# A four-layer graph network on one core: border tiles are kept in SBUF and scattered last, instead of being gathered twice

## The reference

```
L0, four steps:  m = (h @ W_msg.T + b).reshape(n, 4, 128)
                 r = segment_sum(m[src, etype], dst);   h = GRU(r, h)
L1:              pe = relu(edge_w @ pos_w1) @ pos_w2
                 s = segment_sum(pe * x[src] + x[src], dst); agg = s / max(cnt, 1)
                 out = relu(batchnorm(concat(x, agg) @ sage_w + b)) + x
L2:              messages = segment_sum(h[src] @ W_msg.T + b + emb[etype], dst);  h = GRU(messages, h)
L3:              attention over the edges of each node with 8 heads, skip, norm, feed-forward
```

## Time and profile before

| | |
|---|---|
| time, median of 3 runs | 4368.6 us (4366.22 to 4368.82) |
| profiled execution | 4371.13 us, its span 4369.0 us |
| TensorE | 2877.3 us busy, 66% of the span |
| VectorE | 1801.5 us, 41% |
| ScalarE | 442.1 us, 10% |
| GpSimd | 2838.1 us, 65% |
| mean granted TensorE clock | 0.816 |
| gathers | 1612 in L0, 806 in L1 and L2, 416 in L3 |

### The profile page before, as it was taken

One profiled execution on the slowest core, in us unless ns is written; L12 is line 12 of the kernel. 1 busy time (PEld: TensorE's weight loads), 2 busy tenths in 40 slices (PEclk: granted clock), 3 DMA queues, 4 the chain that ended last, 5 costly groups with the idle time before them and its releaser, 6 DMA issues. The chain is left out here.

```text
span 4369.0 us, 45184 instructions
## 1 busy us (share of the span) xinstructions
PE 2877.3 (66%) x12174; PEld 2171.4 (50%) x12175; DVE 1801.5 (41%) x4737; ACT 442.1 (10%) x719; POOL 2838.1 (65%) x2971
## 2 busy tenths in 40 slices
PE   6565576555765567666667777776555866664697
PEld 3444444444444444444446666644444455654574
DVE  5222242222422224444453333432222666667874
ACT  3000020000200002000011111120000211111333
POOL 5777767777677776777746777557777277775000
PEclk9777787777977778877888999977777888887799
DMA  4112221212221222122212111112112155553340
GB/s 168 52 52 52 53 87 52 53 52 52 88 52 53 53 52 87 53 52 52 52 30 70 52 52 52 40 48 52 53 52 52 47 154 157 157 157 108 106 144 15
DMA packets 143872, 313.44 MB, mean 72 GB/s; under 512 B 49875, under 2 KB 64410, under 8 KB 143290
## 3 DMA queue, kind: packets, MB, share of 16 engines
q0 software_dynamic: 97344, 213.17, 18.1%
q1 hardware_dynamic: 46458, 99.48, 6.5%
HBM read 250.83 MB, written 61.63 MB: 72 GB/s over the span
## 5 line engine op out<-in xcount | busy, mean ns | idle before, releaser
L584 POOL DMA_INDIRECT ring<-m_tab,idx x1612 | 1535.0, 952 | 521.5 <-issue 489.6
L1535 PE MATMUL ps<-nodes,ring 128*128 128x256 f32 (+1 forms) x2816 | 897.2, 483 | 509.6 <-DMA ring<-m_tab,idx 399.1
L1535 PE MATMUL ps<-oh,ring 128*128 128x256 f32 (+1 forms) x2852 | 891.3, 476 | 475.9 <-DMA ring<-m_tab,idx 376.7
L1535 PEld LDWEIGHTS ps<-nodes,ring 128*128 128x128 f32 x2816 | 643.8, 252 | 657.8 <-issue 553.0
L1535 PEld LDWEIGHTS ps<-oh,ring 128*128 128x128 f32 x2852 | 647.8, 250 | 625.5 <-issue 518.1
L584 POOL DMA_INDIRECT ring<-x_tab,idx x806 | 766.6, 951 | 254.4 <-issue 238.9
L1022 DVE TENSOR_SCALAR oh<-iota,dl 128x256 f32<-128x256 f32 x1223 | 373.2, 375 | 941.0 <-PE ps L1535 940.3
L1022 DVE TENSOR_SCALAR nodes<-iota,dl 128x256 f32<-128x256 f32 x1200 | 366.7, 376 | 856.0 <-PE ps L1535 856.0
L584 POOL DMA_INDIRECT ring<-kv_tab,idx x416 | 401.3, 965 | 133.2 <-issue 126.5
L594 POOL TENSOR_TENSOR small<-small,bc 128x4 f32<-128x4 f32 (+1 forms) x28 | 29.6, 1057 | 452.5 <-DVE small L1121 452.5
L1535 PE MATMUL ps<-wpad,rts 128*128 128x128 f32 x832 | 157.1, 366 | 179.8 <-DVE pw L1312 179.8
(11 more groups left out here) (257 smaller groups left out, 2524.7 us busy)
## 6 DMA issues: line engine op xcount, KB each, us to landing
ve_dr<-pw SPq DMA_DIRECT2D x52, 512.0 KB, 3.0
ring<-ve_dr SPq DMA_DIRECT2D x52, 512.0 KB, 3.4
ring<-m_tab,idx POOLq DMA_INDIRECT x1612
m_tab<-ring SPq DMA_DIRECT2D x75, 256.0 KB, 2.1
ring<-x_tab,idx POOLq DMA_INDIRECT x806
ring<-kv_tab,idx POOLq DMA_INDIRECT x416
nodes<-in_xT SPq DMA_DIRECT2D x2, 1600.0 KB, 13.5
kv_tab<-nodes SPq DMA_DIRECT2D x25, 128.0 KB, 1.7
```

The costliest lines, as they stand in the source:

```text
L584: pool.indirect_dma_start(rows[:, j, :], None, table, bass.IndirectOffsetOnAxis(ap=idx[:, wave * WV + j:wave * WV + j + 1], axis=0)).then_ ...
L1535: return T.matmul(o, lhsT, rhs, start=start, stop=stop, skip_group_check=True)
```

## The change

The second gather of border tiles goes away: 391 gathers a pass in the six passes before L3.

ScalarE copies every landed tile out of its ring slot into one of 20 places in the half of `ring` that these passes leave free: a tile that crosses a border goes to the place of that border, any other to one of eight places that each wave writes over. The column of the place comes from a table (`kept_at`) over `load_kept`. TensorE waits for a wave's copies (`kept`) before its last tile (in L1, before the second half), so that the credit covers them. In L1 the copies are made of the finished messages, four after each half wave.

Wave 48 now has seven tiles, four on the slot's semaphore and three on `gat_end`. Two waves without gathers follow, 49 with eight border tiles and 50 with four. Their one-hots are built like those of other waves, with buffers of their own for the last waves. Behind the last of them VectorE moves the twelve border tiles to fixed rows (`move_borders`), and TensorE scatters each when it is moved (`borders`), in the order of banks. `evac` no longer waits for the whole pass: bank c goes when border 2c is scattered (`border`), the last with the credit; L1 keeps the old rule. In L0 the first matmul of `gru` waits for banks 0 to 2 only, L2 for all.

At the start TensorE has a matmul more (`later`) and VectorE fourteen steps more, on one partition, that work out the places: two ahead of the border records, twelve behind `i_iob`, ahead of the table adds L1148. Since `kept_at` lies in `cols_b`, the three steps that fill `cols_b` for L3 move from before L2's pass to behind L2's update, ahead of L3's first one-hots.

```diff
-P_WAVES = -(-P_SLOTS // WV)
-P_LAST = P_SLOTS - (P_WAVES - 1) * WV
+M_WAVES = -(-TILES // WV)
+M_LAST = TILES - (M_WAVES - 1) * WV
+M_FIRST = 4
+P_WAVES = M_WAVES - (-P_EXTRA // WV)
...
+        def bank_done(eng, k, c):
+
+            if c == NCH - 1 or l1(k):
+                eng.wait_ge(credit, first_wave(k + 1) + DEPTH)
+            else:
+                eng.wait_ge(border, k * (NCH - 1) + c + 1)
...
             def gathers(k, table, width, idx):
-                waves, deep, slots = (WAVES, RING, SLOTS) if single(k) else (P_WAVES, DEPTH, P_SLOTS)
+                waves, deep, slots = (WAVES, RING, SLOTS) if single(k) else (M_WAVES, DEPTH, TILES)
...
-                        ).then_inc(gat[u], 16)
+                        ).then_inc(gat_end if not single(k) and wave == M_WAVES - 1 and j >= M_FIRST else gat[u], 16)
...
             def evac(k):
-                act.wait_ge(credit, first_wave(k + 1) + DEPTH)
                 for c in range(1, NCH, 2):
                     c0, cw = CH[c]
+                    bank_done(act, k, c)
...
+            def keep(r, j, rows, last=False):
+
+                ins = nc.scalar.activation(ring_flat[:, ds(r[j], P)], rows[:, j, :], ACT.Copy)
+                if last:
+                    ins.then_inc(kept, 1)
+
+            def keep_tiles(k):
+
+                def wave(i, u, g, n):
+                    if isinstance(g, int) and g >= M_WAVES:
+                        return
+                    r = load_kept(act, kept_at, mybir.EngineType.Activation, first_slot(g), n)
+                    arrived(act, k, i, u, g)
+                    act.wait_ge(kept, k * M_WAVES + i * DEPTH + u + 1)
+                    for j in range(n):
+                        if n == M_LAST and j == M_FIRST:
+                            last_arrived(act, k)
+                        keep(r, j, wave_rows(g, u), j == n - 1)
...
             def relus(i, waves):
...
                         nc.scalar.activation(pw[:, hf, :], ps[:, 7, :], ACT.Relu).then_inc(l1_relu, 1)
+                        act.wait_ge(l1_msg, q + 2)
+                        if hf == 0:
+                            act.wait_ge(kept, PASS_L1 * M_WAVES + i * DEPTH + u + 1)
+                        for j in range(4 * hf, min(n, 4 * hf + 4)):
+                            keep(r, j, wave_rows(wave, u), j == n - 1)
...
+            def move_borders(k):
+
+                at = load_kept(dve, border_at, mybir.EngineType.DVE, 0, P_EXTRA)
+                dve.wait_ge(kept, (k + 1) * M_WAVES + 1)
+                for b in range(P_EXTRA):
+                    V.tensor_copy(border_rows(b), ring_flat[:, ds(at[b], P)]).then_inc(moved, 1)
...
+            def borders(k, wave, counting=False):
+
+                u, n, b0 = wave - LOOPED * DEPTH, tiles_of(wave), (wave - M_WAVES) * WV
+                pe.wait_ge(oh_ready, first_wave(k) + wave + 1)
+                for j in range(n):
+                    c0 = (b0 + j + 1) * PAIR
+                    pe.wait_ge(moved, k * P_EXTRA + b0 + j + 1)
+                    ins = mm(psf[:, c0:c0 + PAIR], border_rows(b0 + j), pair_oh(k, u, wave, j), start=False, stop=False)
+                    if (b0 + j) % 2 == 0:
+                        ins.then_inc(border, 1)
...
+                ins.then_inc(credit, 1)
...
             def sums(k, counting=False):
...
+                        if j == n - 1:
+                            tiles_kept(k, i * DEPTH + (u + 1))
...
-            def evacuated(k):
+            def evacuated(k, first=False):
                 def f(c=0):
-                    if c == 0:
+                    if c == 0 and first:
+                        pe.wait_ge(ev_d, k * EV_D + 2)
+                        pe.wait_ge(ev_a, k * EV_A + 1)
+                    elif c == 0 or c == 1 and first:
```

More of the change, by code:

```diff
@@ L83, in load_cols, with load_kept @@
         skip_runtime_bounds_check_because="window starts are multiples of 128 under 3200 by construction")[1]
+def load_kept(eng, row, which, start, n):
+    return eng.bass.values_load_multi_w_load_instructions(
+        row[0:1, ds(start, n)], engines=[which], min_val=P, max_val=(P_EXTRA + WV - 1) * PAIR + P,
+        skip_runtime_bounds_check_because="the column of one of 20 places for tiles")[1]
 def load_both(pe, row, wave):
@@ L116, in tiles_of, with first_slot, in_first @@
 def tiles_of(wave):
-    return P_LAST if isinstance(wave, int) and wave == P_WAVES - 1 else WV
-IN_SLOT = [16 * sum(tiles_of(wave) for wave in range(s, P_WAVES, DEPTH)) for s in range(DEPTH)]
+    if not isinstance(wave, int) or wave < M_WAVES - 1:
+        return WV
+    return M_LAST if wave == M_WAVES - 1 else min(WV, P_EXTRA - (wave - M_WAVES) * WV)
+def first_slot(wave):
+    if not isinstance(wave, int) or wave < M_WAVES:
+        return wave * WV
+    return TILES + (wave - M_WAVES) * WV
+def in_first(wave):
+    return M_FIRST if wave == M_WAVES - 1 else WV
+IN_SLOT = [16 * sum(in_first(wave) for wave in range(s, M_WAVES, DEPTH)) for s in range(DEPTH)]
 def landed(k, s, i, n=WV):
@@ L255, in build @@
         gat = [sem(f"gat{i}") for i in range(max(DEPTH, RING))]
+        gat_end = sem("gat_end")
+        kept = sem("kept")
+        border = sem("border")
+        moved = sem("moved")
         mt_mm = sem("mt_mm")
@@ L372, in build, with pair_oh, l1 @@
         oh_half = [oh[:, b, :, :].rearrange("p s c -> p (s c)") for b in range(2)]
[L373 to L377 removed]
+        oh_half += [gT[:, 1024 * b:1024 * (b + 1)] for b in range(3)] + [rec_flat[:, 3600:4624], oh_x]
+        END_HALVES = {M_WAVES - 1: (4, 6), M_WAVES: (0, 1), M_WAVES + 1: (5,)}
+        def pair_oh(k, u, wave, j):
+            half = 2 * (u % OH_BUFS) + j // 4
+            if isinstance(wave, int) and (wave > M_WAVES or wave >= M_WAVES - 1 and not l1(k)):
+                half = END_HALVES[wave][j // 4]
+            return oh_half[half][:, (j % 4) * PAIR:(j % 4 + 1) * PAIR]
+        def l1(k):
+            return isinstance(k, int) and k == PASS_L1
         def slot(s):
@@ L429, in whole_turns @@
                 turn(i, [i * DEPTH + u for u in range(DEPTH)])
-            turn(LOOPED, [LOOPED * DEPTH + u for u in range(P_REST)])
+            turn(LOOPED, list(range(LOOPED * DEPTH, M_WAVES)))
         def new_state(unit, eng, r, c, h_in, h_out):
@@ L719, in relus @@
                 for u, wave in enumerate(waves):
-                    for hf in halves(wave):
+                    n = tiles_of(wave)
+                    r = load_kept(act, kept_at, mybir.EngineType.Activation, first_slot(wave), n)
+                    for hf in range(2):
                         q = (i * DEPTH + u) * 2 + hf
@@ L985, in _ @@
             step("w_c16", V.tensor_scalar(cols16[:, :], cols2[:, :], 3, None, ALU.arith_shift_right))
+            after_g = pw[0:1, 1, 0:TILES + 1]
+            is_border = pw[0:1, 2, 0:TILES]
+            in_wave = pw[0:1, 3, 0:M_WAVES * WV]
+            n_before, lower, n_lower, none = (small[0:1, q:q + n] for q, n in (
+                (256, P_EXTRA), (272, P_EXTRA * P_EXTRA), (420, P_EXTRA), (436, P_EXTRA)))
+            step("x_n", V.tensor_copy(n_before, ps[0:1, 2, 0:P_EXTRA]))
+            dve.wait_ge(s_pe, PE["later"])
+            step("x_g", V.tensor_copy(after_g[:, 0:TILES], ps[0:1, 0, 0:TILES]))
             dve.wait_ge(s_ac, AC["r_a10"])
@@ L1208, in _ @@
             V.tensor_scalar(rts[:, 0, :], recT[:, 0:P], 0.0, None, ALU.add)
-            pair_hot(0, 0, WV).then_inc(oh_ready, 1)
+            pair_hot(PASS_L1, 0, 0, WV).then_inc(oh_ready, 1)
             def messages(i, waves):
                 for u, wave in enumerate(waves):
-                    for hf in halves(wave):
+                    final = isinstance(wave, int) and wave == M_WAVES - 1
+                    for hf in range(2):
                         if hf:
@@ L1570, in _ @@
             step("off", T.transpose(ps[0:1, 2, 0:P], small[:, 0:1], ident))
+            step("later", mm(ps[0:1, 0, 0:TILES], ones[0:P_EXTRA, 0:1], nodes[0:P_EXTRA, 2, 0:TILES]))
             first_table(1, 2)
@@ L1769, in messages @@
                 pe.wait_ge(l1_msg, (i * DEPTH + u) * 2 + (hf + 2))
+                tiles_kept(PASS_L1, i * DEPTH + (u + 1))
                 scatter(u, hf, cs).then_inc(credit, 1)
             whole_turns(pe, messages)
+            for wave in range(M_WAVES, P_WAVES):
+                borders(PASS_L1, wave)
             evacuated(PASS_L1)()
```

114 lines of the change are left out of this document (85 added, 29 removed).

## The result

The changed kernel takes 4308.3 us (median of four runs, 4302.3 to 4310.5), the kernel before 4367.4 beside it: a ratio of 0.9862, 95% interval 0.9851 to 0.9874, some 59 us faster. The prediction said 4313, 4300 to 4341.

The account below looks back on a forecast made before the run. GpSimd's gathers were taken to bound each pass, with a tail behind the last landing. Gains of 35.7, 8.0, 10.7 and 5.4 less 4.0 make 55.8 us: 4371.13 to 4315.3, less 2.5 for the median, 4313 us (4300 to 4341).

Parts of the forecast that it names:

- L1: L1's pass: with waits for copies a turn takes 39.7 us, inside GpSimd's 40; 5.4 us gained.
- the sum: Whole kernel: 35.7 + 8.0 + 10.7 + 5.4 - 4.0 = 55.8 us gained; chance 0.60 for 4305 to 4321.
- the stages between: Work between and after the gather passes: no term in the forecast, 0 us gained.
- The gathers removed: Six passes before L3: 12 gathers fewer in each, at 1.25 us, save 15.0 us a pass.
- ScalarE's copies cost nothing in a plain pass: Eight copies and a load take idle ScalarE 3.0 us of a 10 us wave; cost taken as nothing.
- The tail of a plain pass: End of a plain pass: update starts at 560.0 instead of 571.95, 11.9 us gained, 35.7 over three passes.
- The clock over the border tiles: Twelve border tiles at granted clock 1.00 take 5.8 us; rival, lower clock in part or whole: 4321 to 4343, chance 0.20.
- L1 falls behind its gathers: Rival in L1: copies at 0.5 us put each of twelve turns 2.9 us over the limit, +35, 4348; chance 0.08.
- the upper level: TensorE's granted clock of 1.00 over the border tiles: 0.487 us a tile, against 0.89 at 0.50.
- The start: Before the first gather: fourteen small VectorE steps that make the places lose 4.0 us (3 to 5.5).

Follow-up runs that it names:

- banks late: The changed kernel with banks copied out only after the last border tile and the update waiting for all of them: 5064.1 us, on a held-up chip.

## Why the prediction was right, and where it was off

The total came out 5 us under the forecast. The mechanism, gathers saved against a new tail, is what the runs show. That the total is so near is in part luck: L1 gave 3.5 us less than the sum said, the other passes 6 more, and the stages between, taken at nothing, 4.2.

**The gathers removed.** Right: 15.0 us a pass by the sum, 15.0 to 15.7 with nothing but the gathers taken away, and 952 to 951 ns each.

**ScalarE's copies cost nothing in a plain pass.** Right, and cheaper than priced: 1.71 us for eight, not 2.5, as the pitch is 0.20 us although one lasts 0.295. Copies with 1.7 times the work cost a plain pass 1.0 to 3.6 us more, on a held-up chip.

**The tail of a plain pass.** Right, step by step. From the last gather's start to the update 11.9 us were predicted (548.10 to 560.0) and 11.17 measured. The landing took 2.86 us from that start, where the row carried over has 2.76 (559.33 to 562.09). TensorE's gap ahead of the border tiles was 1.44 us and not 1.75, since the moves started right behind the one-hots. Twelve border tiles took 5.45 us and not 5.8, and the update started 0.2 us before their end. The passes gained 0.5 to 1.6 us more than the 11.9; the part that the tail does not explain lies in the gathers (488.2 us in the first pass, against 504.0 less 15.0).

**The clock over the border tiles.** Right in the plain passes and in L2 (1.00 behind gaps of 1.44 and 1.46 us), wrong for part of the counting pass (0.79 behind a gap of 2.38 us, with pairs of records of 1.20 us and not 0.68). That pass gained 10.0 all the same. In a second profile of the changed kernel, on the last chip, the same gap of 2.38 us was followed by 1.00, and the tail was 14.7 us and not 16.5.

**L1 is the step that was mis-sized.** The sum had 0.25 us of wait in three waves of a turn and 1.25 at its end, 39.7 us a turn, inside GpSimd's 40. The waits were no larger than that: seven half waves take 4.66 us on average, 0.6 more in a turn than at 4.57 and not 0.75, and a turn's end takes 6.61 us where the clock stays up, and not 6.91. Such a turn is 39.2 us long where it waits for no landing. But behind seven of the twelve turn ends the clock fell (0.71 to 0.74), and eight scatter records, the hidden matmuls and the next ones at the lower level cost some 1.6: 7.9 to 8.4 us at the end, and mostly 40.5 to 41.0 us a turn. The sum priced the wait and not what the clock does after it. L1's last message came 5.2 us later against its first gather (2762.15 less 2258.82, against 2804.46 less 2306.35) and not 1.2, hence 1.9 us gained and not 5.4. This is the rival "L1 falls behind its gathers" at a tenth of its price: it had the thin slack of 0.3 us a turn right, but it priced dearer copies (0.5 us each), and what used up the slack was the clock.

The prediction held the Trainium skill's page "TensorE: Matmul & The Clock Gate", section "HAM oscillation — how this bites in real kernels", against its choice of the upper level. The section does not speak against it: in the kernel that it describes, the waits that send the clock down are longer than the gap of 1.44 us ahead of the border tiles, and longer than the gaps of 1.88 to 2.38 us that the lower clock followed here. The kernel before has such a longer wait, 3.83 us, and its wave from 562.1 began at 0.50, which agrees. The shorter gaps went both ways: those of 1.44 us left the clock up, L1's wait of 1.88 us was followed by 0.71 to 0.74 at seven turn ends of twelve, and the gap of 2.25 us ahead of the update was followed by 1.00 in one pass and by 0.61 in the next of one kernel. One row of such a gap at full clock was not enough to price all of them at full clock.

**The start.** Right in the sum, 3.9 us for 4.0, not in its parts: three narrow steps took 1.2 to 1.4 us, and the twelve stand on VectorE from 46.7 to 53.6, of which only 3.9 us show at the first gather. 2.6 of it came back with the steps behind the adds.

**The stages between.** Predicted at nothing, measured at 4.2, of which 3.1 lie between L2's update and L3's first gather (85.4 before, 82.2 after) and 1.8 behind the counting pass's update. Nothing was put down for what the early banks do to the matmuls behind them, and the runs show it. In the four profiles of kernels whose banks leave late (before, also on a held-up chip; border gathers left out; banks late) the stage behind L2's update takes 84.7 to 85.7 us, with a granted clock of 0.50 to 0.63 in its first 10 us. In the ten with early banks it takes 79.0 to 82.5 us, at 0.66 to 1.00. Banks late differs from the changed kernel in the banks alone, on the same chip: 85.1 us at 0.50 against 81.8 at 0.83. The rest, from 79.0 to 82.5 among kernels that do not differ in this stage, stays open, as does the hold-up on the three chips.

## What to carry to other kernels

A copy engine that stands idle is a cheap way to save a second fetch, if the copies lie behind a landing and ahead of a wait that has slack; where they lie between a message and its scatter, let the consumer wait at the last tile that needs them, not at the first. Price a new wait of a microsecond or two on TensorE twice: once as it is, and once with the work behind it at the lower clock. What only the last landing's tiles release (here four one-hots) is worth building a wave early: 1.0 to 1.6 us a plain pass for one number in a wait. A gap removed ahead of a stretch of matmuls can give back more than its own length, if the stretch then runs at the upper clock.

## What was not expected of the hardware

On three chips both kernels took 16% longer. In the changed kernel every third wave of a plain pass is held up there, with VectorE idle for some 20 us and GpSimd for 4.4; in the kernel before the holds are less regular. The change gained 0.7% there in place of 1.4%. ScalarE's 128x128 copies start every 0.20 us while each is on record with 0.295. The same wait of 1.88 us on TensorE was followed by the lower clock at seven of twelve turn ends in one profile, and at nine in another of the same kernel.
